# VectorE's queue reordered in a fused conditioning, attention and SwiGLU kernel: gate_ffn first in its slot, all scores of the first twelve slots centred

## The reference, cut to what matters

```python
x = layernorm(x) * weight + bias + tanh(cond @ lin_w.T + lin_b)      # then * weight + bias again
h = gamma_a(cond) * rmsnorm(x) + beta_a(cond)
q, k, v = split(h @ W_q.T), split(h @ W_k.T), split(h @ W_v.T)       # 16 heads of 16
o = softmax(scale * q @ k.T) @ v                                     # within a sequence
x = x + alpha_a(cond) * (o @ W_o.T)
h = gamma_f(cond) * rmsnorm(x) + beta_f(cond)
x = x + alpha_f(cond) * ((silu(h @ gate_w.T) * (h @ hidden_w.T)) @ out_w.T + out_b)
```

## Time and profile before

| | |
|---|---|
| median of 3 runs | 1007.26 us (1006.86 to 1007.68) |
| the profiled execution | 1006.64 us |
| its span in the trace | 1004.8 us |
| TensorE busy (matmuls) | 943.0 us, 94% |
| VectorE busy | 719.9 us, 72% |
| ScalarE busy | 623.0 us, 62% |
| GpSimd busy | 581.7 us, 58% |
| DMA | 23.34 MB, 23 GB/s in the mean |

### The profile page before, as it was taken

The page is one execution under the profiler, slowest core; times in us unless marked ns, Lnnn a source line. Parts: engine busy times, 40 slices in busy tenths (PEclk is TensorE's granted clock), DMA queues, the critical chain, the costliest instruction groups (busy, mean ns, idle before and its releaser), DMA issues.

```text
span 1004.8 us, 28386 instructions
## 1 busy us (share of the span) xinstructions
PE 943.0 (94%) x11164; PEld 899.6 (90%) x11164; DVE 719.9 (72%) x1349; ACT 623.0 (62%) x1775; POOL 581.7 (58%) x531
## 2 busy tenths in 40 slices
PE   5566999999999999999999999999999999999998
PEld 5445899999999999999999999999999999999997
DVE  6656777777777777777777777777777776766655
ACT  4555766676566567656656765665667567666432
POOL 4556666757465665746566664656666565544320
PEclk9899999999999999999999999999999999999999
DMA  6000001000010100000010000001000000000000
GB/s 236 17 22 2 23 12 33 6 30 13 13 32 12 33 11 23 12 14 32 12 34 12 23 12 16 30 12 33 12 22 13 12 13 12 12 12 12 12 12 22
DMA packets 20931, 23.34 MB, mean 23 GB/s; under 512 B 1216, under 2 KB 20288, under 8 KB 20800
## 3 DMA queue, kind: packets, MB, share of 16 engines
q1 hardware_dynamic: 20800, 21.54, 6.6%
HBM read 13.15 MB, written 8.39 MB: 21 GB/s over the span
## 4 chain that ended last, share of the span: by engine, by line
PE 89%; DVE 4%; issue 3%; POOL 2%; ACT 1%; DMA 0%; SPq 0%; DVEq 0%; ACTq 0%; POOLq 0%
PE psum L293 18%; PE psum L295 17%; PE psum L294 17%; PE psum L507 6%; PE psum L506 6%; PE psum L505 6%; PE psum L432 5%; PE psum L408 4%; PE psum L448 4%; PE psum L342 2%; PE psum L323 2%; PE psum L501 1%; DVE late L721 1%; PE psum L331 1%; PE psum L335 1%
## 5 line engine op out<-in xcount | busy, mean ns | idle before, releaser
L293 PE MATMUL psum<-xf_hi,ffn_hi 128*128 128x256 f32 x1024 | 289.8, 283 | 2.3 <-ACT probsT L905 1.6
L295 PE MATMUL psum<-xf_hi,ffn_lo 128*128 128x256 f32 x1024 | 285.9, 279 | 0.0
L294 PE MATMUL psum<-xf_lo,ffn_hi 128*128 128x256 f32 x1024 | 285.8, 279 | 0.0
L897 ACT ACTIVATE probs<-psum,least 128x64 f32<-128x64 f32 x976 | 215.7, 354 | 56.6 <-DVE least L632 55.3
L293 PEld LDWEIGHTS psum<-xf_hi,ffn_hi 128*128 128x128 f32 x1024 | 192.2, 188 | 3.6 <-issue 2.6
L1091 POOL TENSOR_TENSOR probs<-probs,inv_sum 128x512 f32<-128x512 f32 x128 | 134.8, 1053 | 104.2 <-DVE inv_sum L653 103.4
L295 PEld LDWEIGHTS psum<-xf_hi,ffn_lo 128*128 128x128 f32 x1024 | 192.4, 188 | 0.0
L294 PEld LDWEIGHTS psum<-xf_lo,ffn_hi 128*128 128x128 f32 x1024 | 192.0, 187 | 0.0
L926 ACT ACTIVATE prod_hi<-late 128x512 fp32r<-128x512 f32 x128 | 83.9, 656 | 136.1 <-DVE late L711 135.9
L507 PE MATMUL psum<-prod_hi,ffn_lo 128*128 128x256 f32 x512 | 143.1, 280 | 0.0
L703 DVE SCALAR_TENSOR_TENSOR late<-tanh,psum 128x512 f32<-128x512 f32 x128 | 87.4, 683 | 77.7 <-ACT tanh L920 77.7
(11 more groups left out here) (106 smaller groups left out, 2217.9 us busy)
## 6 DMA issues: line engine op xcount, KB each, us to landing
out_t_dram<-x_res SPq DMA_DIRECT2D x31, 256.0 KB, 2.2
xin<-x_dram SPq DMA_DIRECT2D x15, 512.0 KB, 4.0
w_raw<-attn_w_dram SPq DMA_DIRECT2D x1, 1024.0 KB, 7.0
x_res<-gate_w_dram SPq DMA_DIRECT2D x1, 1024.0 KB, 9.6
late<-hidden_w_dram SPq DMA_DIRECT2D x1, 1024.0 KB, 11.6
w_raw<-out_w_dram SPq DMA_DIRECT2D x1, 1024.0 KB, 6.4
xin<-x_dram SPq DMA_DIRECT2D x2, 256.0 KB, 2.9
k_heads<-mod_w_dram SPq DMA_DIRECT2D x1, 320.0 KB, 4.7
```

What stands on the lines that cost most here:

```text
L293: pe.matmul(out, stat_hi, mov_hi, start=first, stop=False)
L294: pe.matmul(out, stat_hi, mov_lo, start=False, stop=False)
L295: return pe.matmul(out, stat_lo, mov_hi, start=False, stop=last)
L897: op = act.activation(probs[g % 2][:, h * SEQ:(h + 1) * SEQ], scores[g % 2][:, h // 2, h % 2], ACT.Exp, bias=least[g % 2][:, h:h + 1], sca ...
```

## The change

On VectorE, `gate_ffn` (and `finish_last`, for the last part) is the first thing of a slot with j = 1. All sequences below 12 are wide. For a wide couple, both exponentials stand where that of the even sequence stood; both `invert_sums` follow the couple's centring at once, ahead of `make_residual`, `scale_a`, `scale_f` and `attended_lo`; and both `normalise_probs` stand first in GpSimd's even slot, ahead of its beta, gamma and squares (in slot 0 they stand between `apply_beta_a(1)` and `split_lo_a(1)`). `scale_a(1)` is kept ahead of the sums in slot 0. What is computed is the same.

```diff
         def wide(g):
-            return g < FFN_AT and g % 2 == 0
+            return g < FFN_AT
...
# VectorE
             for s in range(FIRST_SLOT, LAST_SLOT):
                 grp, j, f = s // PSEQ, s % PSEQ, s - FFN_AT
+                if j == 1 and 0 <= grp - 4 < NPART - 1:
+                    gate_ffn(grp - 4)
+                if j == 1 and grp - 4 == NPART - 1:
+                    finish_last(grp - 4)
                 if j == 1 and is_group(grp):
                     mean_squares_out(grp)
...
                             if wide(g):
                                 centre(g)
+                    if s == 0:
+                        scale_a(1)
+                    for g in (s, s + 1):
+                        if is_seq(g) and wide(g):
+                            invert_sums(g)
                 if s == FIRST_SLOT + 2:
                     scale_a(0)
-                if s == 0:
-                    scale_a(1)
...
-                if is_seq(s):
+                if is_seq(s) and not wide(s):
                     invert_sums(s)
                 if j == 2 and is_part(grp - 1):
                     attended_lo(grp - 1)
-                if j == 1 and 0 <= grp - 4 < NPART - 1:
-                    gate_ffn(grp - 4)
-                if j == 1 and grp - 4 == NPART - 1:
-                    finish_last(grp - 4)
...
# ScalarE
                 if wide(g):
-                    act.wait_ge(scores_read, g + 1)
+                    act.wait_ge(scores_read, g + 2)
...
                 if s % 2 == 0 and is_seq(s):
                     exponentials(s)
+                    if wide(s + 1):
+                        exponentials(s + 1)
...
-                if s % 2 == 0 and is_seq(s + 1):
+                if s % 2 == 0 and is_seq(s + 1) and not wide(s + 1):
                     exponentials(s + 1)
...
# GpSimd
                 if s == 0:
                     apply_beta_a(1)
+                for g in (s, s + 1):
+                    if s % 2 == 0 and is_seq(g) and wide(g):
+                        normalise_probs(g)
+                if s == 0:
                     split_lo_a(1)
...
-                if is_seq(s):
+                if is_seq(s) and not wide(s):
                     normalise_probs(s)
```

## The result

The changed kernel takes 997.1 us in the median of 4 runs (995.34 to 998.15), the kernel before 1007.47. The ratio is 0.9895, interval 0.9882 to 0.9908. So it gains 1.0%, clear of the noise and the way that was forecast, but 10.4 us and not 16.5, and it lies 1.1 us above the range of 986 to 996. The profiled execution took 997.22 us with a span of 995.4.

The account below looks back on a forecast made before the run. TensorE was taken as the bound from about 100 us, chains across engines before that. 1006.64 - 18.95 (line 501) + 3.0 (start) = 990.7, beside the median 991.3, stated as 991; range 986 to 996.

Parts of the forecast that it names:

- gate_ffn first: Steady state, slot j = 1: gating fits VectorE's earlier idle, so line 501 stops waiting; gain 18.95 us.
- What is late next: Steady state after the gating move: no other TensorE wait grows; GpSimd's normalising still has 0.71 us left.
- The moved stall: Rival, steady state: gating delays mean squares and so the turn, 9.5 us comes back, 1000 us; chance 0.06 above 995.
- the slower case by late completion: Rival, steady state: down projection's completion reaches VectorE so late that the turn waits longer, 1019 us; chance 0.03.
- The order of the first twelve slots: Start: residual and scaling steps come 2.4 us later per couple, probabilities earlier; about +0.1 us at full clock.
- my sums for TensorE at full clock: Start, couple by couple: changes of +0.9, +1.7, -0.1, +0.4, -1.2 and +0.9 us, about +0.1 taken with full clock.
- the clock's term: Start: TensorE's longer waits (4 to 5 us) bring half clock to matmul passes behind them; sum +3.9, taken as +3.0 us.
- three such passes at half clock: Start: passes of 12 matmuls behind longer waits, each up to 1.4 us more at half clock; sum +3.9.
- the bare idle of 12.3 us: Line 501, steady state: lower bound of the gain, 12.3 us, if the restart cost were an artefact of modelled ends.
- The shorter start: Rival, start: waits for GpSimd's probabilities vanish and the residual chain is no longer, about 4 us gained, 984 us; chance 0.08.

Follow-up runs that it names:

- e1: Kernel before with only gate_ffn and finish_last moved to the front of VectorE's slot, first twelve slots unchanged: 987.85 us, ratio 0.9809.
- e11: Changed kernel with unused TensorE matmuls sized to fit the waits (10 and 14 in slots 0 and 1, 19 before queries, 13 before output projections): 987.32 us, ratio 0.9799.
- e7: e3 with more unused matmuls, 10 in slot 0 and 24 ahead of keys(1): 989.70 us, ratio 0.9836.
- e12: e6's order with unused matmuls refitted: 10 and 9 in slots 0 and 1, 4 ending slot 3, 10 before queries and output projections: 979.88 us, ratio 0.9727.
- e3: Changed kernel with unused matmuls in TensorE's waits, slots 2 to 11 (14 before queries and output projection, 4 ending odd slots): 991.11 us, ratio 0.9837.
- e9: e7 with 20 unused matmuls before queries in place of 14 and none at the end of odd slots: 989.93 us, ratio 0.9815.
- e4: Changed kernel with residual and scaling ahead of row sums on VectorE, and gamma, squares and beta ahead of normalising on GpSimd: 988.75 us, ratio 0.9814.
- e6: e4 with unused TensorE matmuls in slots 2 to 11 (10 before queries and output projections, 2 ending odd slots): 981.83 us, ratio 0.9755.
- e10: e6's order with unused matmuls as in e9, but 10 ahead of queries and output projections: 983.51 us, ratio 0.9752.
- e8: Changed kernel with only GpSimd's order undone, both normalisings again behind gamma, squares and beta: 993.34 us, ratio 0.9870.
- e5: e1 with unused TensorE matmuls in slots 2 to 11 (10 before queries and output projections, 2 ending odd slots): 986.94 us, ratio 0.9812.

## Why the prediction was wrong

The steps one by one. *gate_ffn first*: right in mechanism and size; 19.3 us in the traces and 20.2 in e1, for 18.95. The idle that the wait view shows, 12.3 us, was too little, so the distance between starts was the right price. *What is late next*: nothing, as said; there is no wait of line 432 or 293 in the steady state that was not there before. *The moved stall* and *the slower case by late completion* don't occur: in both kinds of group the mean squares start 2.51 or 2.52 us before the last matmul of `hidden` does, as they did before (311.94 and 314.45 then, 317.71 and 320.22 now); only in the second part and in the last ones are they 0.1 to 0.6 us later, and line 501 waits there for nothing either.

*The order of the first twelve slots*: the intervals between the `find_least` of successive couples, in us, with my sums for TensorE at full clock:

| couples | before | changed | forecast, full clock | e11 |
|---|---|---|---|---|
| 0 to 2 | 13.10 | 15.23 | 14.0 | 12.67 |
| 2 to 4 | 10.41 | 12.62 | 11.2 | 12.62 |
| 4 to 6 | 13.45 | 13.32 | 11.65 | 11.77 |
| 6 to 8 | 10.03 | 13.55 | 10.5 | 10.55 |
| 8 to 10 | 13.04 | 13.54 | 11.8 | 12.03 |
| 10 to 12 | 12.03 | 14.08 | 12.95 | 12.49 |
| sum | 72.06 | 82.34 | 72.1 | 72.13 |

The last four couples, where e11 ran at full clock, are met within 0.5 us, three of them within 0.25. The first two are off by 1.3 and 1.4 in opposite directions: I had carried over keys(1) at half clock, which e11 has at full clock, and e11's only half-clock stretch (3.4 us) fell mostly on the second; in e7 that couple took 11.72 us without it, so 0.5 of the 1.4 is left. So the new order, held at full clock, costs +0.1 against the old order at the clock that it had, as I had summed: e11 takes 987.3 us beside e1's 987.9, whose start had 20.5 us at half clock. What the old order would take at full clock no run shows.

The step that failed is the clock's term. I wrote "with three such passes at half clock, less the two half-clock stretches that now hit the turns, the sum is +3.9", and took +3.0. The table has 10.3 us (and as the changed execution came to its slot 0 0.4 us earlier, 9.9 at line 501); 1006.64 - 19.3 + 9.9 = 997.2 is the profiled time. find_least(12) came at 110.5 us, for "101 to 104.5", and the scores of couple 6 3.8 us later, for "about where they are". I had named the right trigger and four of the right waits, but priced only the 12 matmuls behind each wait. The half clock went on over what followed: over the output projection, the turn, the values, the scores, the transposes (from 74.1 to 84.3 us without a break), where all of it lies on the couple's chain. Couple 6 to 8 shows it: the output projection starts 5.58 us after find_least(6), as forecast (5.6); the turn comes 1.35 us later than forecast, which is the pass that I had priced; and turn, values and scores add 1.7 us for which I had nothing. Together these are the 3.05 us between 13.55 and 10.5. And it came at two waits for which I had counted none, ahead of keys(1) (3.7 us, 2.5 before) and of the turn in slot 4 (3.7, 2.6 before); couple 0 to 2 has 10.2 us of half clock where it had 3.7. The changed start has 34 us more of half clock than the old one and is 10.3 us longer.

The range was too narrow for two reasons. It did not hold its own bounds together: the bare idle of 12.3 us with +3.9 gives 1006.64 - 12.3 + 3.9 = 998.2. And with the right gain at line 501 no price of the clock that I had worked out comes near: +3.9 gives 991.6, and even all four passes at their full 1.4 us, 5.6 on top of +0.1, give 993.4, where the execution took 997.2.

Not every microsecond at half clock costs the same. e1's start had 6.8 us more of it than the kernel before and was 0.3 us longer (72.34 for 72.06), while 34 us more cost 10.3 in the changed kernel. The kernel before shows the clock's cost with no edit at all: of its 28 executions beside the experiments, the five with a granted clock of 0.991 or 0.992 had a median of 1005.4 us, the seven with 0.982 or 0.983 one of 1008.9. That is 3.5 us for some 18 us more at half clock.

*The shorter start* as a rival did not come true in this order, but its ground was sound: with the residual and scaling steps ahead of the row sums and the clock held up, the start takes 64.8 us (e12, find_least(0) to find_least(12)) for 72.1 in the kernel before and in e11.

The Trainium skill's rule on idle stretches (TensorE: Matmul & The Clock Gate, "HAM oscillation — how this bites in real kernels") pointed the right way. I had read it as +4 in place of +3, because I counted passes and not what followed them. The runs agree with the rule itself: the start shrinks as work without use is put into the waits, from 82.3 us to 76.0 (e3), 76.1 (e7), 74.4 (e9) and 72.1 (e11), and in the order of e4 from 73.5 to 65.6 (e6), 68.1 (e10) and 64.8 (e12). In e7, e9 and e10 the fillers that did not fit took part of the gain back.

Not settled: how much of the 10.3 us belongs to VectorE's and how much to GpSimd's order, since e8 changed the clock as well. What e11's order would gain or lose against the old one with both at full clock is open too, since e5's start kept 13.7 us at half clock. That each half-clock stretch is caused by the longer waits is shown for the whole (e3, e11), not stretch by stretch.

## What to carry to other kernels

A wait that only one VectorE instruction ends, with that engine idle shortly before, was worth its full distance between TensorE starts here (1.03 against 0.35 us), not the idle that the wait view shows (0.45), and the forecast could be taken at face value because the instruction fitted into the earlier idle. Where TensorE is busy for about half of the time, as in this start, an order that lengthens its waits can have two prices: its own, which a walk along the chain gave within 0.5 us in five couples of six, and the half clock, which falls on everything that TensorE does next on the chain (a turn of 1.94 us for 1.07), not only on the one pass behind the wait. Give such a stretch a bound worked out with all of its matmuls at half clock, and look at the granted clock by windows before believing a start's length.

## What the runs showed of the hardware that I had not expected

Matmuls without any use, 0.24 us each, made the kernel faster: in e3 TensorE was busy 57.6 us from 28 to 100 us, against 43.2 in the changed kernel, and the time fell by 6 us (991.1 against 997.1). In e11 and e12 the start ran at a granted clock of 0.95 to 1.00 with TensorE busy 62 and 59 of 72 us (28 to 100 us), against 43 of 72 and 0.70 to 0.79 in the changed kernel. A matmul of 128 x 128 in float32 by the identity shows as two records of 0.12 us (13 written, 26 in the row at 67.19). And fillers were only free where they fitted into the wait: ahead of keys(1), where the changed kernel waited 3.7 us, 24 of them (5.5 us) held it back by 1.5 us, and 14 (3.3 us) left 0.57 us of the wait.
